# Layer 1 attention takes the value product of a batch one step later, behind the next scores; layer 0 folds its score scale into the latents

## Chip, cores and metric

One core of one Trainium2 chip runs the whole program: one launch, float32 inputs and outputs in HBM. The metric is the device time of a run in microseconds (us), and its median over several runs. The engines are called PE (matrix products; PEld is its load of stationary weights), DVE (VectorE), ACT (ScalarE), POOL (GpSimd) and SP (it issues the DMAs).

## The reference, cut to what matters

Two transformer layers after each other on a float32 stream x; each adds attention, normalises, adds a feed-forward part and normalises. The change touches the two attentions.

```python
# layer 0: 4 x 256 tokens, 32 heads, keys and values from a latent of 64, no mask
q  = (x @ Wq_c.T + bq_c) @ Wq_up.T + bq_up          # 192 latents for the queries
kv = x @ Wkv_c.T + bkv_c                            # 64 latents and 64 rope columns
scores = einsum(q, [kv_nope @ Wk_up.T, kv_rope]) / sqrt(192)
out = softmax(scores) @ v ; out = out @ Wo.T + bo
# layer 1: 4 batches x 256 tokens, 32 heads of 128, causal mask
q, k, v = x @ wq, x @ wk, x @ wv                    # per head 128 columns
scores = where(causal, q @ k.T * 192**-0.5, -1e30)
out = (softmax(scores) @ v) @ wo
```

The reference's causal mask is over 256 tokens of a batch, so of a batch's four 128 x 128 blocks of scores three are computed.

## The kernel before, in words

Every float32 operand of PE is split into a part `hi` rounded to fp32r and a rest `lo`, and a product is three matmuls (`matmul3`, L106 to L108): hi x hi, lo x hi, hi x lo. A split takes ACT for `hi` and DVE (or POOL) for `lo`. All engines have a queue of their own, in an order that is written out by hand, and meet by counting semaphores.

**Layer 0.** `attention0_heads` goes through 32 heads in rounds of four (one per batch); heads 2 to 26 run in a loop. For each head PE first multiplies the up-projection of queries and keys together (`merge`, two small float32 products in PSUM bank `bq`, L900). DVE then scaled the bank by 1/sqrt(192) into SBUF tile `gm` (`merged_raw`, L745), POOL scaled the rope columns into the other half of `gm` (`rope_part`, L603), ACT rounded `gm` to `gm_hi` (`merged`, L665) and DVE took `gm_lo` (`merged_lo`, L759). PE's `query` (L106 to L108, L913, L914) multiplies these weights with the query latents into `bq`; ACT and DVE split its result (`h_q_hi` L670, `h_q_lo` L763). Scores (`h_bs`) are products with the split latents `a_kv`. In the prologue the order is: latents, `merge(0)`, `query(0)`, scores, `merge(1)`.

**Layer 1.** `Attention1.programs` runs 32 heads x 4 batches = 128 steps s = 4h + t. Heads go in quads q (0 to 7); u = 0 to 15 is the step within a quad. Quads 1 to 6 are one hardware loop (`Fori`), quads 0 and 7 stand apart. In step s PE did, in this order:

1. scores of s+1 (five matmuls into `c_bs`, L106 to L108, L2462, L2463),
2. `turn`: three transposes of the probabilities of s (`c_bt`, L75), which wait for ACT's `normalise` of s (L1962),
3. products of the next head (`c_bx`, `c_by`), of the next quad's values (`c_bv`, `c_bw`: v1 to v7) and of the output projection,
4. values of s (five matmuls into `c_bo`, L106 to L108, L2481, L2483), which wait for the `lo` split of the probabilities (L2147) and for the value weights `c_v_lo` (`corner_lo`, L2178).

DVE's order in step s was: `out_sum(s-1)` (L2153, adds two halves of the output in `c_bo`), some of the value splits (`corner_lo`), `maxes(s+1)` (L2131, L2132, L2135, L2137, L2139), `outs(s-1)` (L2160), `probs(s)` (L2147), `inverse(s+1)` (L2143), then sums of the products. ACT's order was: `out_rest(s-1)` (L1972), value splits `corner_hi` (L2003), `probs(s)` (L1967), `outs(s-1)` (L1978, waits for `out_sum(s-1)`), value splits and copies `value_copy` (L2003, L1993), `exps(s+1)` (L1954, waits for `maxes`), copies of products (L2009), `normalise(s+1)` (L1962), `sum_hi` (L2016). PE's product v6 of a quad's second value pair stands in step u = 0 and waits for `value_copy(.., 0)`, v7 in u = 1 for `value_copy(.., 1)`.

The functions that the diff touches follow.

Of the kernel before, what the change touches and what calls it, by code (L numbers as in the profile page):

```python
# [34 lines left out]
ALU = mybir.AluOpType  # L35
# [178 lines left out]
class Latents0:  # L214
# [103 lines left out]
    def latent_hi(self, act, i):  # L318
# [4 lines left out]
        if m == 2:  # L323
# [4 lines left out]
            act.activation(self.kv[0][:, tok], self.kvraw[:, tok], ACT.Identity).then_inc(self.s_hi, 1)  # L328
# [5 lines left out]
    def latent_lo(self, dve, i):  # L334
# [94 lines left out]
def attention0_heads(nc, k, io, g, lat, acc, first, tail, norm, ffn, after, attn1, layer1):  # L429
# [13 lines left out]
    with ExitStack() as ctx:  # L443
# [7 lines left out]
        gm = t.sb("gm", [P, 2, P])  # L451
# [17 lines left out]
        s_gmm, s_graw, s_gpool, s_ghi, s_glo = (k.sem(x) for x in ("g_mm", "g_raw", "g_pool", "g_hi", "g_lo"))  # L469
# [52 lines left out]
        def merged_weights(h):  # L522
            i = tail_index(h)
            return (gms, gb) if i is None else (tail["gms"][i], tail["gb"][i])

# [18 lines left out]
        with nc.Block() as block:  # L544
# [49 lines left out]
            def _(pool):  # L594
                def rope_part(h):

                    _, _, rope, _ = weights(h)
                    loaded(pool, h)
# [60 lines left out]
            def _(act):  # L659
                def merged(h):  # L660
                    act.wait_ge(s_graw, h + 1)
                    act.wait_ge(s_gpool, h + 1)
                    if not is_late(h):
                        need(act, s_qmm, 2 * h)
                    act.activation(merged_weights(h)[0][0][:, :, :], gm[:, :, :], ACT.Identity).then_inc(s_ghi, 1)  # L665
# [58 lines left out]
                exps(0, 0)  # L724
                lat.latent_hi(act, 5)
                lat.rows_hi(act, 1)
                query(1, 1, 0)
                merged(1)
# [13 lines left out]
            def _(dve):  # L742
                def merged_raw(h):
                    dve.wait_ge(s_gmm, h + 1)
                    dve.tensor_scalar(gm[:, :, 0:KVL], bq[:, 0:2 * KVL].rearrange("p (a n) -> p a n", a=2), SCALE0,  # L745
                                      None, ALU.mult).then_inc(s_graw, 1)

                def merged_bias(h):
# [3 lines left out]
                    dve.scalar_tensor_tensor(out=terms[:, :], in0=factors[:, 0, :], scalar=SCALE0,  # L752
# [3 lines left out]
                def merged_lo(h):  # L756
                    hi, lo = merged_weights(h)[0]
# [2376 lines left out]
```

## Time and profile before

| | us |
|---|---|
| median of 3 runs (lowest, highest) | 1400.92 (1398.64, 1401.22) |
| the profiled execution | 1398.13 |
| its span in the trace | 1396.1 |
| outside the span | 2.0 |

PE is busy 99% of the span, DVE 75%, ACT 65%, POOL 62%. Layer 0's attention takes the first 363 us of the span, its feed-forward part the time to 490, layer 1's attention that to about 1320, and the last feed-forward part the rest. The clock granted to PE is that of full speed throughout. A matmul is shown with the time from its start to its modelled end, so that neighbours overlap; what one costs is the distance from start to start.

### The profile page before, as it was taken

What the parts mean: (1) busy time and instruction counts of PE and PEld (TensorE: products, weight loads), DVE (VectorE), ACT (ScalarE), POOL (GpSimd) and SP (SyncE); (2) the same over time, 40 slices, a digit from 0 to 9 for tenths busy, and PEclk for the clock granted to TensorE, in tenths of its full rate; (3) what the DMA queues carried; (4) which work ended last, traced back from release to release, by engine and by line L of the source; (5) the groups of instructions that cost most, each with busy time, mean ns of one, the idle gap of its engine ahead of it and who ended that gap; (6) DMA issues with size and microseconds to landing.
All of it is one profiled execution on the core that took longest, in us unless ns stands there. A gap on an engine that the chain in (4) does not pass through costs nothing.

```text
span 1396.1 us, 29891 instructions
## 1 busy us (share of the span) xinstructions
PE 1381.8 (99%) x8601; PEld 1216.0 (87%) x8601; DVE 1046.3 (75%) x2570; ACT 905.1 (65%) x2487; POOL 859.9 (62%) x926
## 2 busy tenths in 40 slices
PE   9999999999999999999999999999999999999998
PEld 7899889988788889898898898898898898898887
DVE  5999999999878886667667667667667667667876
ACT  5888888888555566566566566576576566566621
POOL 3655555555131367886885885886886886885521
PEclk9999999999999999999999999999999999999999
DMA  5533333322344400111102102102102002101201
GB/s 193 166 97 93 100 93 96 97 71 56 110 143 140 147 16 31 61 32 61 45 18 64 42 16 73 33 16 75 30 16 75 30 16 75 30 16 44 86 16 46
DMA packets 61299, 93.00 MB, mean 67 GB/s; under 512 B 6176, under 2 KB 31520, under 8 KB 61216
## 3 DMA queue, kind: packets, MB, share of 16 engines
q1 hardware_dynamic: 61072, 91.93, 22.2%
q8 instruction: 31, 0.51, 0.1%
q14 instruction: 52, 0.43, 0.1%
q10 hardware_dynamic: 144, 0.13, 0.0%
HBM read 81.82 MB, written 2.10 MB: 60 GB/s over the span
## 4 chain that ended last, share of the span: by engine, by line
PE 86%; DVE 5%; issue 3%; POOL 3%; ACT 3%; DMA 0%; POOLq 0%; DVEq 0%; ACTq 0%; SPq 0%
PE h_bo L949 5%; PE c_bx L106 4%; PE c_bx L108 4%; PE c_bv L106 4%; PE c_bx L107 4%; PE c_bv L108 3%; PE c_bv L107 3%; PE h_bo L1452 3%; PE a_acc L1452 3%; PE c_by L106 3%; PE c_bw L106 3%; PE c_by L108 3%; PE c_by L107 3%; PE h_bt L75 3%; PE c_bw L108 3%
## 5 line engine op out<-in xcount | busy, mean ns | idle before, releaser
L623 POOL TENSOR_TENSOR h_pr<-h_pr,h_rinv 128x512 f32<-128x512 f32 x128 | 133.4, 1042 | 136.4 <-DVE h_rinv L774 134.1
L1879 POOL TENSOR_TENSOR c_qk<-g_y,c_qk 128x512 fp32r<-128x512 f32 x96 | 123.4, 1296 | 100.8 <-ACT c_qk L2016 94.1
L1677 POOL TENSOR_TENSOR b_sw_lo<-b_slots,b_sw_hi 128x512 fp32r<-128x512 f32 (+1 forms) x128 | 151.1, 1180 | 10.3
L1675 POOL CAST b_sw_hi<-b_slots 128x512 fp32r<-128x512 f32 (+1 forms) x128 | 73.9, 577 | 90.1 <-DMA b_slots<-in_w_qk 69.3
L676 ACT ACTIVATE h_pr<-h_bs,h_nmax 128x256 f32<-128x256 f32 x256 | 119.6, 481 | 2.5 <-DVE h_nmax L769 2.4
L1962 ACT ACTIVATE c_pr<-c_pr,c_rinv 128x128 f32<-128x128 f32 (+1 forms) x256 | 101.8, 448 | 13.3 <-DVE c_rinv L2143 13.3
L2016 ACT ACTIVATE c_qk<-g_y 128x512 fp32r<-128x512 f32 x96 | 60.1, 628 | 72.6 <-DVE g_y L2203 72.1
L2153 DVE TENSOR_TENSOR c_bo<-c_bo,g_wo 128x128 f32<-128x128 f32 x128 | 38.3, 299 | 84.1 <-ACT g_wo L1972 69.7
L1632 POOL TENSOR_TENSOR b_slots<-b_slots 128x256 f32<-128x256 f32 x128 | 96.1, 773 | 2.5
L1954 ACT ACTIVATE c_pr<-g_wo,c_nmax 128x128 f32<-128x128 f32 x128 | 51.5, 403 | 63.6 <-DVE c_nmax L2139 63.6
L769 DVE TENSOR_REDUCE h_nmax<-h_bs 128x2 f32<-128x512 f32 x128 | 87.5, 683 | 0.0
L778 DVE TENSOR_TENSOR h_pt_lo<-h_bt,h_pt_hi 128x512 fp32r<-128x512 f32 x128 | 87.1, 680 | 0.3
L1967 ACT ACTIVATE c_pt<-c_bt 128x384 fp32r<-128x384 f32 x128 | 62.7, 489 | 31.6 <-PE c_bt L75 30.3
L1972 ACT ACTIVATE g_wo<-c_bo 128x128 f32<-128x128 f32 x128 | 34.5, 270 | 72.3 <-PE c_bo L2483 72.3
L106 PE MATMUL c_bx<-b_ts,b_sw_hi 128*128 128x512 f32 x192 | 78.9, 411 | 0.2
L682 ACT ACTIVATE h_pt_hi<-h_bt 128x512 fp32r<-128x512 f32 x128 | 76.4, 597 | 0.0
L106 PE MATMUL h_bs<-a_kv_hi,h_q_hi 128*128 128x256 f32 x256 | 74.6, 292 | 0.9 <-ACT h_pr L676 0.5
L108 PE MATMUL c_bx<-b_ts,b_sw_lo 128*128 128x512 f32 x192 | 75.4, 393 | 0.0
L949 PE MATMUL h_bo<-h_pt_hi,a_cs 128*128 128x256 f32 x252 | 75.1, 320 | 0.3 <-DVE h_o_mix L783 0.2
L107 PE MATMUL c_bx<-b_ts,b_sw_hi 128*128 128x512 f32 x192 | 75.0, 390 | 0.0
L75 PEld LDWEIGHTS h_bt<-g_ident,h_pr_t 128*128 128x128 f32 x512 | 54.9, 140 | 20.3 <-issue 7.8
L108 PE MATMUL h_bs<-a_kv_hi,h_q_lo 128*128 128x256 f32 x256 | 71.7, 280 | 0.0
(521 smaller groups left out, 5472.6 us busy)
## 6 DMA issues: line engine op xcount, KB each, us to landing
f_wi<-in_w_ffn SPq DMA_DIRECT2D x66, 256.0 KB, 2.7
b_slots<-in_w_qk SPq DMA_DIRECT2D x64, 256.0 KB, 3.0
a_w<-in_w_head SPq DMA_DIRECT2D x28, 352.0 KB, 3.0
h_part<-in_w_ffn SPq DMA_DIRECT2D x32, 264.0 KB, 2.7
h_o_mix<-h_o_hi SPq DMA_DIRECT2D x62, 128.0 KB, 2.2
b_vw_lo_raw<-in_w_v SPq DMA_DIRECT2D x9, 512.0 KB, 4.7
c_v_raw<-in_w_o SPq DMA_DIRECT2D x8, 512.0 KB, 4.1
g_xT_raw<-in_w_o SPq DMA_DIRECT2D x8, 512.0 KB, 4.0
```

What stands on the lines that cost most here:

```text
L75: return pe.transpose(out.bitcast(F32R), rows, ident)
L106: pe.matmul(out, w[0], x[0], start=start, stop=False, skip_group_check=True)
L107: pe.matmul(out, w[0], x[1], start=False, stop=False, skip_group_check=True)
L108: return pe.matmul(out, w[1], x[0], start=False, stop=stop, skip_group_check=True)
L623: pool.tensor_tensor(pr[b][:, :, :], pr[b][:, :, :], rinv[b][:, :][:, :, None].to_broadcast([P, 2, S]), ALU.mult)\
L676: m = act.activation(pr[b][:, i, :], bs[b % 2][:, i * S:(i + 1) * S], ACT.Exp, bias=nmax[b][:, i:i + 1], accum_out=rsum[b][:, i:i + 1])
L769: dve.tensor_reduce(nmax[b][:, :], bs[b % 2][:, :].rearrange("p (a n) -> p a n", a=2), AX, ALU.max, negate=True).then_inc(s_max, 1)
L949: m = pe.matmul(out, cs[:, 2 * (2 * c + b % 2) + kt, :], pt[b][j][:, kt, :], start=(b % 2 == 0 and kt == 0 and j == 0), stop=(kt == 1 and ...
L1632: pool.tensor_tensor(slot(out), slot(a), slot(b), op).then_inc(self.s_comb, 1)
L1677: pool.tensor_tensor(self.sw[1][:, a:b], self.slots[:, a:b], f32(self.sw[0][:, a:b]), ALU.subtract)\
L1879: pool.tensor_tensor(lo, y[:, (0, 2, 1)[i], :], f32(hi), ALU.subtract).then_inc(s_sumlo, 1)
L1962: m = act.activation(x[:, cols], x[:, cols], ACT.Identity, scale=rinv[t % 2][:, i:i + 1])
```

## The change

Layer 1: values of s-1 stand in step s, behind scores(s+1) and ahead of the turn, in all quads but the last, and there for u = 0; from u = 1 of the last quad on the old order holds. Their wait for the value weights (`values_ready`) moves with them. DVE takes `maxes(s+1)` first and `out_sum(s-1)` behind them; `value_total(2q-1, 2)` (L2173) goes from the start of step u = 3 to the end of u = 2.

Layer 0: the scale 1/sqrt(192) is applied to the latents (ACT's `scale=`, DVE's `scalar_tensor_tensor`), so `merged_raw` and tile `gm` go; ACT and DVE split the bank `bq` itself (64 instead of 128 columns for each of the two halves), and POOL splits the rope columns with two instructions in place of one. PE's `query` waits for POOL too. Head 1 uses a tail head's buffers, and its merge is split earlier in the prologue.

```diff
-            act.activation(self.kv[0][:, tok], self.kvraw[:, tok], ACT.Identity).then_inc(self.s_hi, 1)
+            act.activation(self.kv[0][:, tok], self.kvraw[:, tok], ACT.Identity, scale=SCALE0).then_inc(self.s_hi, 1)
...
-            dve.tensor_tensor(self.kv[1][:, tok], self.kvraw[:, tok], f32(self.kv[0][:, tok]),
-                              ALU.subtract).then_inc(self.s_lo, 1)
+            dve.scalar_tensor_tensor(out=self.kv[1][:, tok], in0=self.kvraw[:, tok], scalar=SCALE0,
+                                     in1=f32(self.kv[0][:, tok]), op0=ALU.mult, op1=ALU.subtract)\
+               .then_inc(self.s_lo, 1)
...
+            if isinstance(h, int) and h == 1:
+                return tail["gms"][0], gb
...
-                    need(pool, s_glo, h)
                     if tail_index(h) is None and is_late(h):
-                        need(pool, s_qlo, 2 * h)
+                        need(pool, s_qmm, 2 * h)
+                    if isinstance(h, int) and h == TAIL0:
+                        pool.wait_ge(s_qmm, 4)
-                    pool.tensor_scalar(gm[:, :, KVL:P], rope, SCALE0, None, ALU.mult).then_inc(s_gpool, 1)
+                    pool.tensor_copy(hi, rope).then_inc(s_rope, 1)
+                    pool.wait_ge(s_rope, h + 1)
+                    pool.tensor_tensor(lo, rope, f32(hi), ALU.subtract).then_inc(s_gpool, 1)
...
-                    act.wait_ge(s_graw, h + 1)
-                    act.wait_ge(s_gpool, h + 1)
-                    if not is_late(h):
-                        need(act, s_qmm, 2 * h)
-                    act.activation(merged_weights(h)[0][0][:, :, :], gm[:, :, :], ACT.Identity).then_inc(s_ghi, 1)
+                    act.wait_ge(s_gmm, h + 1)
+                    act.activation(from_merge(merged_weights(h)[0][0]), merged_bank, ACT.Identity)\
+                       .then_inc(s_ghi, 1)
...
-                def merged_raw(h):
-                    dve.wait_ge(s_gmm, h + 1)
-                    dve.tensor_scalar(gm[:, :, 0:KVL], bq[:, 0:2 * KVL].rearrange("p (a n) -> p a n", a=2), SCALE0,
-                                      None, ALU.mult).then_inc(s_graw, 1)
...
-                    dve.tensor_tensor(lo[:, :, :], gm[:, :, :], f32(hi[:, :, :]), ALU.subtract).then_inc(s_glo, 1)
+                    dve.tensor_tensor(lo, merged_bank, f32(hi), ALU.subtract).then_inc(s_glo, 1)
...
                     pe.wait_ge(s_glo, h + 1)
+                    pe.wait_ge(s_gpool, h + 1)
...
-                    if has(s - 1, NSTEP):
+                    late = not is_last(q) or u == 0
+                    if has(s - 1, NSTEP) and not late:
                         out_sum(s - 1)
...
-                    if filled and u == 3:
-                        value_total(2 * q - 1, 2)
...
                     if has(s + 1, NSTEP):
                         maxes(s + 1, (t + 1) % 4)
+                    if has(s - 1, NSTEP) and late:
+                        out_sum(s - 1)
...
                     add(1)
+                    if filled and u == 2:
+                        value_total(2 * q - 1, 2)
...
                         scores(s + 1, (t + 1) % 4)
+                    if late and has(s - 1, NSTEP):
+                        if u == 0:
+                            pe.wait_ge(s_clo, corners(2 * q - 2, "22"))
+                        else:
+                            values_ready(q, u - 1)
+                        values(s - 1, (j - 1) % 4 if t == 0 else j, (t - 1) % 4)
...
-                    values(s, j, t)
+                    if is_last(q):
+                        values_ready(q, u)
+                        values(s, j, t)
```

## Rows read from the trace of the kernel before

**Rows 1.** The page, part 1: busy us (share) xinstructions.

```profile
PE 1381.8 (99%) x8601; PEld 1216.0 (87%) x8601; DVE 1046.3 (75%) x2570; ACT 905.1 (65%) x2487; POOL 859.9 (62%) x926
```

**Rows 2.** Busy time by windows: layer 0's loop, layer 1's loop.

```profile
100.00:200.00 100.00, 100.00 (x733) 90.07 (x733) 93.84 (x209) 83.43 (x247) 53.90 (x69) 1.00 0.36 95
...
700.00:800.00 100.00, 99.85 (x613) 88.55 (x612) 67.20 (x183) 63.02 (x181) 78.30 (x81) 1.00 0.12 38
```

**Rows 3.** Waits of PEld: us in total, times, longest.

```profile
PEld c_bo L106 <- DVE c_v_lo L2178: 3.9, 7, 0.6
```

**Rows 4.** Timeline 12 to 22.5: start us, us, engine, line, operation [idle before].

```profile
18.29 0.29 DVE L745 TENSOR_SCALAR h_gm<-h_bq 128x128 f32<-128x128 f32 x1
18.40 0.39 PE L108 MATMUL h_bt<-g_xT_hi,p_wlo 128*128 128x512 f32 x1
...
19.06 0.43 DVE L759 TENSOR_TENSOR h_gm_lo<-h_gm,h_gm_hi 128x256 fp32r<-128x256 f32 x1 [0.48 <-ACT h_gm_hi L665]
...
19.64 0.47 PE L106 MATMUL h_bq<-a_qa_hi,h_gm_hi 128*128 128x512 f32 x1 [0.85 <-DVE h_gm_lo L759]
```

**Rows 5.** The page, part 5: groups of instructions.

```profile
L2153 DVE TENSOR_TENSOR c_bo<-c_bo,g_wo 128x128 f32<-128x128 f32 x128 | 38.3, 299 | 84.1 <-ACT g_wo L1972 69.7
```

**Rows 6.** Timeline of a late prologue stretch, 22 to 46.

```profile
31.44 0.79 DVE L759 TENSOR_TENSOR h_gm_lo<-h_gm,h_gm_hi 128x256 fp32r<-128x256 f32 x1
...
35.56 0.35 PE L106 MATMUL h_bs<-a_kv_hi,h_q_hi 128*128 128x256 f32 x1 [0.32 <-ACT h_pr L676]
```

**Rows 7.** Timeline of layer 0's loop, 200 to 215.

```profile
201.23 0.53 POOL L603 TENSOR_SCALAR h_gm<-a_w 128x128 f32<-128x128 f32 x1
...
204.31 0.39 PE L106 MATMUL h_bq<-a_qa_hi,h_gm_hi 128*128 128x512 f32 x1
```

**Rows 8.** Timeline of a plain step of layer 1, 750 to 771.

```profile
755.26 0.28 PE L106 MATMUL c_bo<-c_pt,c_v_hi 128*128 128x256 f32 x1
...
755.79 0.33 PE L106 MATMUL c_bs<-c_qk 128*128 128x256 f32 x1
```

**Rows 9.** Timeline of step u = 3 of a quad; last row one quad later.

```profile
742.12 0.39 PE L108 MATMUL c_bw<-g_xT_hi,c_oT 128*128 128x512 f32 x1
...
742.66 0.38 PE L106 MATMUL c_bo<-c_pt,c_v_hi 128*128 128x256 f32 x1 [0.15 <-DVE c_v_lo L2178]
742.72 0.80 ACT L1962 ACTIVATE c_pr<-c_pr,c_rinv 128x128 f32<-128x128 f32 x2 [0.78 <-DVE c_rinv L2143]
...
743.87 0.41 PE L75 MATMUL c_bt<-g_ident,c_pr_t 128*128 128x128 f32 x3
...
845.87 0.39 PE L108 MATMUL c_bw<-g_xT_hi,c_oT 128*128 128x512 f32 x1
```

**Rows 10.** Timeline of steps u = 15 and u = 0, 812 to 829.

```profile
817.84 0.79 ACT L1962 ACTIVATE c_pr<-c_pr,c_rinv 128x128 f32<-128x128 f32 x2
...
819.17 0.41 PE L75 MATMUL c_bt<-g_ident,c_pr_t 128*128 128x128 f32 x3
...
821.12 0.30 DVE L2153 TENSOR_TENSOR c_bo<-c_bo,g_wo 128x128 f32<-128x128 f32 x1 [2.46 <-issue]
...
822.09 0.63 ACT L2003 ACTIVATE c_v_hi<-c_vy 128x512 fp32r<-128x512 f32 x1 [0.24 <-DVE c_vy L2173]
...
823.21 0.40 ACT L1954 ACTIVATE c_pr<-g_wo,c_nmax 128x128 f32<-128x128 f32 x1
...
825.04 0.28 PE L106 MATMUL c_bv<-b_vw_hi,b_ts 128*128 128x256 f32 x1
```

**Rows 11.** The end of quad 0: ACT and PE in time.

```profile
610.41 0.80 ACT L1962 ACTIVATE c_pr<-c_pr,c_rinv 128x128 f32<-128x128 f32 x2
...
611.26 0.46 PE L75 MATMUL c_bt<-g_ident,c_pr_t 128*128 128x128 f32 x3
```

**Rows 12.** The instructions of L2178: ns min/median/max, first and last start.

```profile
L2178 DVE TENSOR_TENSOR c_v_lo<-g_y,c_v_hi x28: 691/786/1371, 594.0 to 1254.5; 128x512 fp32r<-128x512 f32 x28
L2178 DVE TENSOR_TENSOR c_v_lo<-c_bv,c_v_hi x14: 677/684/692, 610.5 to 1255.8; 128x512 fp32r<-128x512 f32 x14
```

More of the change, by code:

```diff
@@ L468, in attention0_heads @@
         s_w, s_wv, s_tick = first["w_in"], first["wv_in"], g["tick"]
-        s_gmm, s_graw, s_gpool, s_ghi, s_glo = (k.sem(x) for x in ("g_mm", "g_raw", "g_pool", "g_hi", "g_lo"))
+        s_gmm, s_rope, s_gpool, s_ghi, s_glo = (k.sem(x) for x in ("g_mm", "rope", "g_pool", "g_hi", "g_lo"))
         s_gb = k.sem("g_b")
@@ L523, in merged_weights, with from_merge, from_rope @@
             i = tail_index(h)
+            if isinstance(h, int) and h == 1:
+                return tail["gms"][0], gb
             return (gms, gb) if i is None else (tail["gms"][i], tail["gb"][i])
+        def from_merge(x):
+            return x[:, :, 0:KVL]
+        def from_rope(x):
+            return x[:, :, KVL:P]
+        merged_bank = bq[:, 0:2 * KVL].rearrange("p (a n) -> p a n", a=2)
         def loaded(eng, h):
@@ L751, in merged_bias @@
                         need(dve, s_qlo, 2 * h)
-                    dve.scalar_tensor_tensor(out=terms[:, :], in0=factors[:, 0, :], scalar=SCALE0,
+                    dve.scalar_tensor_tensor(out=terms[:, :], in0=factors[:, 0, :], scalar=1.0,
                                              in1=factors[:, 1, :], op0=ALU.mult, op1=ALU.mult,
@@ L756, in merged_lo @@
                 def merged_lo(h):
-                    hi, lo = merged_weights(h)[0]
+                    hi, lo = (from_merge(x) for x in merged_weights(h)[0])
                     dve.wait_ge(s_ghi, h + 1)
-                    dve.tensor_tensor(lo[:, :, :], gm[:, :, :], f32(hi[:, :, :]), ALU.subtract).then_inc(s_glo, 1)
+                    dve.tensor_tensor(lo, merged_bank, f32(hi), ALU.subtract).then_inc(s_glo, 1)
                 def query(p, par, h):
@@ L798, in round_ @@
                         maxes(s, b)
-                    if is_late(fresh):
-                        merged_raw(fresh)
                     if isinstance(s, int) and s == 1:
@@ L861, in _ @@
                     lat.latent_lo(dve, i)
-                merged_raw(0)
                 merged_lo(0)
@@ L869, in _ @@
                 maxes(0, 0)
-                merged_raw(1)
                 inverse(0, 0)
+                merged_lo(1)
                 lat.latent_lo(dve, 5)
@@ L874, in _ @@
                 query(1, 1, 0)
-                merged_lo(1)
                 lat.rows_lo(dve, 1)
@@ L2563, in v3, with values_ready @@
                     value_product(to, self.VS4, tokens(1, 1), pair, bw, False, s_vy)
+                def values_ready(q, u):
+                    head, b = divmod(u, 4)
+                    if is_first(q):
+                        pe.wait_ge(s_clo, (NB if head >= 2 else 0) + b + 1)
+                    else:
+                        which = ("11", "12", "21", "22")[head // 2 * 2 + b // 2]
+                        pe.wait_ge(s_clo, corners(2 * q - 2 + b % 2, which))
                 for t in range(NB):
                     s, u = 4 * h + t, 4 * j + t
+                    late = not is_last(q) or u == 0
                     if has(s + 1, NSTEP):
@@ L2573, in unit @@
                         scores(s + 1, (t + 1) % 4)
+                    if late and has(s - 1, NSTEP):
+                        if u == 0:
+                            pe.wait_ge(s_clo, corners(2 * q - 2, "22"))
+                        else:
+                            values_ready(q, u - 1)
+                        values(s - 1, (j - 1) % 4 if t == 0 else j, (t - 1) % 4)
                     ahead = isinstance(s, int) and s == 0
@@ L2644, in unit @@
                             out_last(i)
-                    if is_first(q):
-                        pe.wait_ge(s_clo, (NB if j >= 2 else 0) + t + 1)
-                    else:
-                        pe.wait_ge(s_clo, corners(2 * q - 2 + t % 2, ("11", "12", "21", "22")[j // 2 * 2 + t // 2]))
-                    values(s, j, t)
+                    if is_last(q):
+                        values_ready(q, u)
+                        values(s, j, t)
             def epilogue():
```

6 lines of the change are left out of this document (3 added, 3 removed).

## The prediction

> **What bounds the kernel now.** First the page's part 1 [rows 1]: PE is busy 1381.8 of 1396.1 us, so at most 14.3 us of the span are open gaps, and no edit here takes a matmul away or adds one. Then busy time by windows [rows 2]: PE fills 100.00 of 100 us in layer 0's loop and 99.85 in layer 1's. DVE is at 94 and 67, ACT at 83 and 63. Work taken from DVE or ACT is therefore worth nothing by itself; only a wait of PE pays. The views of waits name two that this change can reach. One stands before layer 0's first query: 0.85 us for DVE's `gm_lo` [rows 4]. The other comes seven times, once in each of the quads 1 to 7: the weights of the value product wait for `c_v_lo`, 3.9 us in all for the weight load [rows 3]. What such a wait costs PE is read from starts [rows 9]: the last product before it starts at 742.12 and a 512-column matmul takes 0.23 from start to start, so the values were due at 742.35; they start at 742.66 and, slowed by the late load, lose 0.1 more: 0.42 us a quad. Third, the timeline around each place, to see what is queued behind what.
>
> **Layer 0, the first query.** `gm_lo` ended at 19.49 and PE started at 19.64; its chunk ended at 18.40 + 0.23 = 18.63 [rows 4]. DVE reached `merged_raw` at 18.29, with its latent splits behind it. Now ACT can round the bank long before that, and DVE goes from 18.29 (a few hundredths later, as one latent split becomes the three-operand form) straight to `merged_lo`, on 128 elements a partition from PSUM: 0.30 by the nearest row [rows 5], so it ends at 18.65 and PE starts at 18.80. Gain 0.84. PE is the bound from there on (the next wait of the prologue stands behind ACT's split of a query, which moves along), so it is kept. ACT's instruction there gets smaller too, off this path.
>
> **Layer 0, the rest.** Head 1's `gm_lo` took 0.79 at 31.44, between a query's split and the maxima that later rounds wait for [rows 6]; the new order does it some 5 us sooner, when DVE is idle. PE loses about 1.2 us in short waits from 35 to 51, of which the 0.32 before 35.56 for the exponentials is one [rows 6]. Part of them sits behind ACT's split of a query, which waits for PE itself. I take 0.4, bounds 0 and 1.2. In the loop nothing is won: POOL's rope part takes 0.53 at 201.23 and the query needs it at 204.31 [rows 7]. Two instructions in place of one, 0.53 each at most and a semaphore between, are ready by 202.5; they no longer wait for DVE's query split. DVE's saving of 0.29 + 0.1 a head stands where it waits for PE anyway.
>
> A rule bears on the 0.79. The Trainium skill (SBUF — State Buffer, "SBUF: two separate sides") says that a DVE instruction with two SBUF inputs and a POOL one that reads SBUF lock each other out of a shared port pair for the whole instruction. By that rule, the new `merged_lo`, with one input in PSUM, is never held up; the trace agrees so far as the 0.79 stands against 0.43 at 19.06. The sum would be the same.
>
> **Layer 1: what the swap does to PE.** Values cost 755.79 - 755.26 = 0.53 [rows 8], and scores 0.59. Scores now start 0.53 sooner, values 0.59 later, the turn when it did. The corner's weights get 0.59 us more, against a wait of 0.42: the stall at u = 3 can go. That is the gain on offer: quads 1 to 6, 6 x 0.42 = 2.5 us (quad 7 keeps the old order there).
>
> **What it does to DVE and ACT.** `out_sum(s-1)` now stands behind `maxes(s+1)`, and ACT's `outs(s-1)` waits for it. ACT's queue is in order, so what stands behind `outs`, value copies and `exps(s+1)`, starts only after maxima + 0.30 (out_sum) + 0.04 + 0.30 (outs): 0.64 after the maxima instead of 0.04, so 0.6 later. In a plain step DVE waited for the scores, and their 0.53 gives that back: nothing is lost. It isn't given back where DVE waits for something else:
>
> - u = 15: DVE waits for ACT's `corner_hi("22")` ahead of the maxima. `exps`, `corner_hi("21")`, `corner_lo("21")` and `normalise` come about 0.52 later (0.6, less the slack that ACT has before the maxima's end). `normalise` ended at 818.63 and the turn started at 819.17 [rows 10]: 0.54 to spare, so even.
> - u = 0: after the loop's end DVE's next instruction came at 821.12, 2.46 after the last [rows 10]; now it comes 0.52 later, at 821.64. From 821.12 to the exponentials at 823.21 lay out_sum (0.25 of DVE's time), value_total and the maxima (1.8) and 0.04; so the maxima end at 823.44. out_sum 0.30 less an overlap of 0.08, 0.04 and outs 0.30: 824.00. Only then come ACT's `corner_hi("12")` and value copy, which ran beside the maxima before and took 823.21 - 822.09 = 1.12: the copy ends at 825.12. PE's product v6 was due at 825.04 [rows 10]. With 0.05 of semaphore: a new wait of 0.15. `exps` start at 825.1 instead of 823.21; I estimate that this just meets the next turn.
> - u = 1: inherits about 1.1, adds its own 0.6 and the copy in front; v7's copy ends just when PE comes: 0.1.
> - u = 2: PE's pace catches up; 0.02.
> - u = 3: value_total has gone, so the maxima start 0.7 sooner, but outs and `corner_hi("12")` now follow them. `c_v_lo`, `inverse` and `normalise` end 0.45 later. `normalise` ended at 743.52 [rows 9], so now at 743.97, and the turn starts at 744.02. In place of 743.87: 0.15 later per quad, with the stall of 0.42 gone and the three small ones in.
>
> So one wait is traded for four: +0.15 x 6 = +0.9. Quad 7's u = 0 gets v6's wait and keeps its old stall: +0.2. At the end of quad 0 `normalise` ends at 611.21 and the turn starts at 611.26, with nothing to spare [rows 11]; 0.52 later there is +0.5. Inside quad 0 the turns are as before.
>
> Bounds for a quad: -0.42 if the four new waits are nil; upwards, `c_v_lo` with both inputs in SBUF takes 0.69 to 1.37, while the one from PSUM never goes over 0.69 [rows 12]. What POOL does beside it is worth up to 0.68, and where I let it run free (u = 0) it may not be: +0.15 + 0.68 = +0.83.
>
> **Sum.** -0.84 - 0.4 + 0.9 + 0.2 + 0.5 = +0.4 us on the profiled execution's 1398.13. That run lies 2.8 below the median of the three, so I set the change against the median: 1401.3.
>
> **Rivals.**
> - *The stall goes and nothing comes in its place.* DVE's slack in u = 0 and u = 1 is larger than I make it, for instance if its 2.46 us at the loop's end shrink when it arrives later. -0.84 - 0.8 - 2.5 + 0.2 = -3.9: 1397.0. For it: the waits that I estimate are of 0.02 to 0.3 us, and each rests on a chain of some eight durations. Against: the order of ACT's queue, which holds whatever the durations are.
> - *Slower: POOL blocks `c_v_lo` at u = 0 or 3 for a whole instruction*, with exps and normalise behind it. It decides once `c_v_lo` ends over 0.3 us later than I have it in every quad. 6 x 0.83 = 5.0, with +0.2 + 0.5 - 1.24: +4.5, so 1405.4. For it: 1.37 is in the trace; against: the other engine's instruction must start just before, and the median is 0.79 [rows 12].
> - *No effect in layer 1.* Values and scores both wait for things that were mostly ready, so the swap may be idle and the corner's stall reappear at the next turn, to the same amount. Then only layer 0 shows: -1.2, 1399.7.
>
> **Chances and range.** My sum 0.35, no effect in layer 1 0.18, stall gone 0.25, POOL's block 0.22. A measurement of this kernel can tell about 0.2% (2.8 us) from no change. The first two lie within it, with little outside: faster 0.27, same 0.51, slower 0.22. The range runs from the stall-gone case, 1397, to near the blocked one, 1405.
>
> **What would show it.** After: no PE wait for `gm_lo` at 19 us, query some 0.8 earlier; no wait of `c_bo` for `c_v_lo` in quads 1 to 6 and one left in quad 7; exps 0.6 after the last maximum instead of 0.04, ACT waiting for `c_bo L2153` ahead of `outs`; new PE waits in u = 0 and 1 (`c_bv` for ACT's copy) and at the turn of u = 4. The loop's period was 103.8 us a quad (742.12 to 845.87, the same product in two quads [rows 9]); I expect 103.9 to 104.0. It is wrong if that period falls by 0.3 or more, or rises by over 0.5.

## The result and the profile after

| | before | after |
|---|---|---|
| median, us (lowest, highest) | 1399.45 (1397.33, 1401.22), 6 runs | 1406.28 (1405.41, 1408.2), 6 runs |
| profiled execution | 1398.13 | 1408.2 |
| its span | 1396.1 | 1406.2 |

The ratio is 1.0056, 95% interval 1.0046 to 1.0067: **slower by 0.56%**, 6.8 us by the medians. The prediction was 1401.3 in a range of 1397 to 1405. It missed, on the side of too little harm, and by more than the two times show: the median that I started from, 1400.92, lay 1.5 above that of the six runs, so the change was forecast at +0.4 and is +6.8.

The page of the changed kernel, parts 1 and 3 (part 3: packets, MB, share), with the one line of the kernel before that answers to the last, behind it. Most lines of layer 1 stand 4 further down than in the kernel before.

```profile
PE 1385.9 (99%) x8601; PEld 1214.9 (86%) x8601; DVE 1030.0 (73%) x2538; ACT 890.1 (63%) x2487; POOL 867.3 (62%) x958
...
q14 instruction: 77, 0.63, 0.1%
```

```profile
q14 instruction: 52, 0.43, 0.1%
```

DVE and ACT have less to do than in [rows 1], and the kernel is slower: the work taken away stood beside PE. What is new is on queue 14, which fetches instructions: 25 packets more, 0.20 MB.

Waits of PE and of its weight load in layer 1 (us in total, times, longest), changed kernel:

```profile
PE c_bw L106 <- DVE c_vy L2177: 3.6, 5, 0.8
PE c_bs L106 <- issue: 0.9, 1, 0.9
PE c_bv L106 <- ACT c_vy L1997: 0.4, 1, 0.4
```

```profile
PEld c_bs L106 <- DVE c_qk L2213: 2.9, 6, 0.5
PEld c_bv L106 <- ACT c_vy L1997: 2.2, 6, 0.9
PEld c_bt L75 <- ACT c_pr L1966: 2.1, 9, 0.4
...
PEld c_bo L106 <- DVE c_v_lo L2182: 0.6, 1, 0.6
```

The corner's wait of [rows 3] is down from seven times to the one of quad 7, as forecast. The first line is the one that I had not seen coming: product v2, at u = 0, waits for `value_total(2q-2, 2)`, five times, as often as the loop returns. The third is v7 in quad 1. (The quoted expectations say TensorE for PE.)

The place where the loop returns, changed kernel (start, us, operation, [idle before]); [rows 10] is the same place before:

```profile
824.65 0.28 ACT L1976 ACTIVATE g_wo<-c_bo 128x128 f32<-128x128 f32 x1 [2.01 <-issue]
...
825.41 0.69 DVE L2177 TENSOR_TENSOR c_vy<-c_bw,c_vy 128x512 f32<-128x512 f32 x1 [3.22 <-issue]
826.23 0.38 PE L106 MATMUL c_bw<-b_vw_hi,g_xT_hi 128*128 128x256 f32 x1 [0.70 <-DVE c_vy L2177]
826.94 0.49 ACT L1971 ACTIVATE c_pt<-c_bt 128x384 fp32r<-128x384 f32 x1 [2.02 <-issue]
```

"issue" means that nothing in the profile holds the engine. DVE's 2.46 us have become 3.22, and ACT, which passed the loop's return without a gap before, stands still for 2.01 and 2.02 us.

Layer 0's first query is as forecast: `gm_lo` takes 0.29, and PE starts 0.90 us sooner than in [rows 4] (I had 0.84). PE keeps that lead through layer 0's attention (0.83 us at 183 us, 0.92 at 337), but layer 1's first value product starts 0.37 later than before, not sooner: the lead is gone by then. What took it was not looked for.

```profile
18.35 0.29 DVE L766 TENSOR_TENSOR h_gm_lo<-h_bq,h_gm_hi 128x128 fp32r<-128x128 f32 x1
...
18.74 0.47 PE L106 MATMUL h_bq<-a_qa_hi,h_gm_hi 128*128 128x512 f32 x1
```

**Quads.** From here on a quad's length is the time from its first value product to the next quad's (starts of `c_bo<-c_pt,c_v_hi` on PE); a wait of PE is the excess of a start-to-start distance over what the same pair of matmuls usually takes. Quads 1 to 5 end with the loop's return; their mean is shown.

| kernel | median | ratio to before (95% interval) | quad 0 | quads 1 to 5 | PE waits in a quad of 1 to 5 |
|---|---|---|---|---|---|
| before | 1399.45 | | 99.8 | 103.85 | u=3: 0.31 |
| changed | 1406.28 | 1.0056 (1.0046, 1.0067) | 100.9 | 105.35 | u=4: 0.49, u=7: 0.23, top: 0.74 to 1.00 |
| e1 layer 0 only | 1398.41 | 0.9999 (0.9989, 1.0009) | 99.8 | 103.87 | u=3: 0.30 |
| e2 layer 1 only | 1402.92 | 1.0027 (1.0017, 1.0037) | 100.7 | 104.73 | u=4: 0.48, u=7: 0.22, top: 0.24 |
| e3 layer 0 only, shifted | 1398.69 | 0.9997 (0.9988, 1.0006) | 99.6 | 104.04 | u=3: 0.31 |
| e4 changed, shifted | 1402.92 | 1.0027 (1.0017, 1.0037) | 100.3 | 104.68 | u=4: 0.5, u=7: 0.23, top: 0 to 0.35 |
| e5 v2 later | 1406.80 | 1.0044 (1.0030, 1.0058) | 100.8 | 105.38 | as changed, but v6: 0.78 to 0.92 |
| e6 v2 later, shifted | 1402.63 | 1.0017 (1.0008, 1.0026) | 100.3 | 104.70 | u=4: 0.47, u=7: 0.21 |
| e7 sum first, shifted | 1402.38 | 1.0017 (1.0008, 1.0026) | 100.3 | 104.54 | u=3: 0.39, u=4: 0.53, u=7: 0.22 |
| e8 late at u=3 only | 1398.66 | 0.9988 (0.9979, 0.9997) | 99.6 | 104.05 | u=3: 0.33 |
| e9 corner first | 1398.94 | 1.0003 (0.9994, 1.0012) | 100.9 | 104.03 | u=7: 0.23, top: 0 to 0.26 |
| e10 exps first | 1400.47 | 1.0013 (1.0004, 1.0022) | 100.0 | 103.62 | u=7: 0.21 |
| e11 corner, exps, v2 | 1399.76 | 1.0008 (0.9999, 1.0017) | 100.2 | 103.55 | u=7: 0.22 |
| e12 late at u=4 only | 1397.59 | 0.9995 (0.9986, 1.0004) | 99.6 | 103.81 | u=4: 0.31 |
| e13 ACT's code shifted | 1406.89 | 1.0059 (1.0046, 1.0073) | 101.1 | 105.27 | as changed |
| e14 DVE's code shifted | 1403.29 | 1.0037 (1.0023, 1.0050) | 100.6 | 104.50 | u=4: 0.47, u=7: 0.21, top: 0 to 0.37 |
| e15 repaired, shifted | 1395.62 | 0.9983 (0.9973, 0.9992) | 100.0 | 103.26 | none |
| e16 repaired | 1395.40 | 0.9975 (0.9966, 0.9984) | 100.4 | 103.49 | none (one quad 104.34) |
| e17 repaired, keys of quad 0 first | 1395.35 | 0.9978 (0.9968, 0.9987) | 100.1 | 103.76 | none (two quads of 104.5) |
| e18 value sum back, shifted | 1402.36 | 1.0031 (1.0019, 1.0042) | 100.7 | 104.45 | u=4: 0.49, u=7: 0.22, top: 0 to 0.25 |

"Before" was measured anew with each group of runs (medians of 1398.33 to 1400.12), so kernels of different groups are compared by their ratios.

In some executions one or two quads carry 0.5 to 0.9 us more at u = 15 or at the top; such a one is in e3, e8, e16, e17 and others, with every order. It stays unexplained.

### The profile page after: what moved, and what is told of

It is laid out like the page before. It is cut to its first block, busy times and chain, and to the rows that moved or that the text cites. A ratio compares the mean times of both kernels' runs of the same rounds, so it can differ in the third digit from the quotient of the medians.

```text
span 1406.2 us, 29858 instructions
## 1 busy us (share of the span) xinstructions
PE 1385.9 (99%) x8601; PEld 1214.9 (86%) x8601; DVE 1030.0 (73%) x2538; ACT 890.1 (63%) x2487; POOL 867.3 (62%) x958
## 4 chain that ended last, share of the span: by engine, by line
PE 83%; DVE 5%; issue 4%; ACT 4%; POOL 3%; DMA 1%; DVEq 0%; SPq 0%; POOLq 0%; ACTq 0%
PE h_bo L953 5%; PE c_bx L106 4%; PE c_bv L106 4%; PE c_bx L108 4%; PE c_bx L107 3%; PE c_bv L108 3%; PE c_bv L107 3%; PE c_bw L106 3%; PE c_bw L108 3%; PE c_bw L107 3%; PE c_by L106 3%; PE h_bt L75 3%; PE c_by L108 3%; PE a_acc L1456 3%; PE c_by L107 3%
## 5 line engine op out<-in xcount | busy, mean ns | idle before, releaser
L1982 ACT ACTIVATE c_oT<-c_bo 128x256 fp32r<-128x256 f32 x124 | 47.8, 386 | 67.4 <-DVE c_bo L2157 65.9
L2164 DVE TENSOR_TENSOR c_oT<-c_bo,c_oT 128x256 fp32r<-128x256 f32 x124 | 52.5, 424 | 51.1 <-ACT c_oT L1982 51.1
L2013 ACT ACTIVATE g_y<-c_bx 128x512 f32<-128x512 f32 x96 | 57.1, 595 | 24.3 <-PE c_bx L108 18.4
```

## The experiments

**Which half of the change.** Theory S: the new order of the steps costs. Theory P: the place of the code does, that is, at which instruction number of an engine's program the loop begins. Counted in the built programs, the layer 0 part takes 8 instructions each out of ACT's and of DVE's program ahead of layer 1's loop.

> The change's layer 0 part alone (the scale taken with the latents, the merge without its raw copy), layer 1 as before. The changed kernel lost 6.8 us; its trace shows, at each return of layer 1's loop, ScalarE idle for 2.0 and 2.3 us where it had not been idle before, VectorE's idle time grown from 2.46 to 3.3 us, and 10 instruction fetches of 8 KB in a period of 105.35 us instead of 5 in 103.75. Theory P (place of the code): the layer 0 part takes 8 instructions each out of ScalarE's and VectorE's programs ahead of layer 1's loop, and so shifts the loop against the fetched blocks. Then this kernel, too, shows ScalarE's new gaps and 10 fetches a period, and the median is 2 to 6 us above the kernel before. Theory S (order of the steps): the loss comes from layer 1's new order. Then this kernel shows 5 fetches and no gap on ScalarE, and lies 0 to 1.5 us below the kernel before.

> The change's layer 1 part alone (value product of a step behind the next step's scores, VectorE's maxima first, one value sum a step sooner), layer 0 as before. ScalarE's program then stands at its old place. Theory P: no gap on ScalarE at the loop's return, about 5 fetches a period, period 103.6 to 104.2 us, median within 2 us of the kernel before. Theory S: the period is 105.0 to 105.5 us as in the changed kernel, TensorE still waits 0.7 to 1.0 us for c_vy at the top of a quad, and the median is 6 to 9 us above the kernel before.

For e3 and e4, "shifted" is this edit, in ACT's and in DVE's prologue of layer 1:

```diff
                 copy(1, 0)
+                for _ in range(16):
+                    act.wait_ge(s_khi, 1)
...
                 inverse(0, 0)
+                for _ in range(16):
+                    dve.wait_ge(s_exp, 1)
```

(16 waits that have long been met; in the built program they are 8 instructions, two waits in each.)

> As the layer 0 part alone, with 16 waits that are long met (8 instructions) added to ScalarE's and to VectorE's program at the end of layer 1's prologue, so that layer 1's loop stands at the instruction number that it has in the kernel before. Theory P: ScalarE's gaps and the extra fetches of the layer 0 part alone are gone, and the median is 0 to 1.5 us below the kernel before, or level with it. Theory S: it is equal to the layer 0 part alone within 0.5 us, whichever way that goes.

> The changed kernel with the same 8 instructions of met waits added to ScalarE's and to VectorE's program ahead of layer 1's loop. Theory P: ScalarE's gaps at the loop's return are gone and the fetches fall from 10 to about 5 a period, VectorE's gap is back at 2.3 to 2.5 us, TensorE's wait for c_vy at the top of a quad falls from 0.9 to 0 to 0.3 us, the period is 103.6 to 104.2 us, and the median is 5 to 9 us below the changed kernel. Theory S: the period stays at 105.0 to 105.5 us and the median stays within 1 us of the changed kernel's 1406.3.

Both theories hold, one for each half. Eight instructions that do nothing made the changed kernel 3.4 us faster (1406.3 to 1402.9), and e2, with layer 0 as before, runs at the same 1402.9. The rest, 3.4 us over the kernel before, is the order. Layer 0's part alone shows ACT's gaps and 10 fetches a quad too (before: 5), but costs nothing: its quads are of 103.87, so with the old order PE does not wait for the engine that comes late. Its forecast gain of 1.2 us (medians: 1.15 and 0.87 under before) is less than these runs tell from none.

**Where the late engine is waited for.** v2 moved behind `p2`, a product of the next head, in the changed kernel and in the shifted one:

```diff
-                    if filled and u == 0:
-                        v2(q, 1)
...
                         (p2, p5, p3)[t](h + 1)
+                    if filled and u == 0:
+                        v2(q, 1)
```

> The changed kernel (its code at its own place, ScalarE's gaps kept) with one edit: TensorE's product v2 at the top of a quad stands behind p2 instead of ahead of it, some 1.3 us later. Shifting the code alone gave 3.4 us. Theory V: the price of the place of the code is paid at one wait, v2's for the last value sum of the quad before (0.74 to 1.00 us a quad, five times in the loop), and nowhere else. Then this edit gives back 4 to 6 us, to 1400.5 to 1402.5, with 10 fetches a period still in the trace, and c_vy's wait on TensorE is gone. Theory W: ScalarE's gaps also make the exponentials and so the turns late; then v2's wait goes but 0.3 to 0.6 us a quad come back at a turn (c_bt waiting for ScalarE's c_pr), and the median is 1403 to 1405.

> The changed kernel with the code shifted to its old place and v2 behind p2. With the shift alone 0.17 us a quad were left at v2 and 1402.9 us in all. Theory V: it falls by 0.17 x 7, to 1401.3 to 1402.2, and the rest of the loss (0.5 us a quad at the turn of the quad's fifth step, 0.23 us at the scores of its eighth, 0.18 us at its thirteenth) stands. A rival: the same 0.2 us comes back one product later, at v6's wait for the value copy, and the median does not move (within 0.5 us of 1402.9).

Theory V's gain did not come, and W's place was wrong: e5's quads are as long as the changed kernel's (105.38 and 105.35). The wait went to v6, next in line, which needs ACT's copy of v1:

```profile
933.08 0.38 PE L106 MATMUL c_bv<-b_vw_hi,b_ts 128*128 128x256 f32 x1 [0.73 <-ACT g_y L1997]
```

So the whole chain of the quad's top is late (DVE's total, the maxima, the output sum, then ACT's output copy, corner and value copy), and not one product.

**Whose code.** Only one engine's program shifted:

> The changed kernel with the 8 instructions of met waits in ScalarE's program alone. Theory 1 (ScalarE's program is the one that lies badly): its gaps of 2.0 and 2.3 us at the loop's return go, the fetches fall from 10 to 5 a period, TensorE's wait at the top of a quad falls from 0.9 to 0.2 us, and the median is that of the kernel shifted on both engines, 1402 to 1403.5. Theory 2 (VectorE's program is): nothing changes, 1405.5 to 1407, 10 fetches.

> The changed kernel with the 8 instructions in VectorE's program alone. Theory 1: 10 fetches and ScalarE's gaps stay, VectorE's gap stays at 3.2 to 3.3 us, since two engines that fetch at once wait longer; the median stays at 1405.5 to 1407. Theory 2: VectorE's gap is back at 2.4 to 2.5 us and the median at 1402 to 1403.5.

Theory 1, which I had favoured, fell. With ACT's shifted (first block) its gaps are gone, the packets are back at 52, and the time does not move; with DVE's shifted (second block) ACT keeps gaps of 1.73 and 1.80, queue 14 has 77 packets, and the 3.4 us are back.

```profile
821.39 0.28 ACT L1976 ACTIVATE g_wo<-c_bo 128x128 f32<-128x128 f32 x1
821.55 0.50 ACT L1971 ACTIVATE c_pt<-c_bt 128x384 fp32r<-128x384 f32 x1
824.09 0.69 DVE L2179 TENSOR_TENSOR c_vy<-c_bw,c_vy 128x512 f32<-128x512 f32 x1 [3.04 <-issue]
824.91 0.38 PE L106 MATMUL c_bw<-b_vw_hi,g_xT_hi 128*128 128x256 f32 x1 [0.51 <-DVE c_vy L2179]
```

```profile
821.36 0.28 ACT L1976 ACTIVATE g_wo<-c_bo 128x128 f32<-128x128 f32 x1 [1.73 <-issue]
821.58 0.69 DVE L2177 TENSOR_TENSOR c_vy<-c_bw,c_vy 128x512 f32<-128x512 f32 x1 [2.41 <-issue]
822.40 0.38 PE L106 MATMUL c_bw<-b_vw_hi,g_xT_hi 128*128 128x256 f32 x1
823.43 0.49 ACT L1971 ACTIVATE c_pt<-c_bt 128x384 fp32r<-128x384 f32 x1 [1.80 <-issue]
```

What costs is the 0.5 to 0.8 us that DVE's gap grows by. ACT's 3.5 to 4.3 us of standing still at each return and its extra fetches, by far the louder signal, lie where ACT has time.

**The turn of u = 4.** The value sum's place and the output sum's place, each taken back alone on the shifted kernel:

> The changed kernel, code shifted to its old place, with VectorE's output sum back ahead of the maxima, TensorE's new order kept. My step in the prediction: the sum behind the maxima makes ScalarE's output copies and exponentials about 0.6 us later. Theory A (the sum's place is the cause): the turn's wait of 0.5 us a quad goes, and the median falls to 1399 to 1401. Theory B (TensorE's order is the cause): the sum now waits for a value product that stands behind the scores, 0.8 to 0.9 us later than the maxima could have begun; maxima, exponentials and turns come that much later in every step, and the median rises by 2 to 40 us over 1402.9, depending on how many of the 128 steps have less slack than that.

> The changed kernel, code shifted to its old place, with one layer 1 edit undone: VectorE's third value sum stands again at the head of the fourth step instead of at the end of the third. It waits for the same product either way and in the trace it began right at that product's end in both, so its 0.67 us should stand in the same place: quads of 104.4 to 104.6 us and a median within 1 us of the shifted kernel's 1402.9. If the sooner sum is what makes the fourth step fit at all, then without it the maxima of the fourth step come 0.2 to 0.7 us later, TensorE waits that much more at the fifth step's turn, and the median is 1404 to 1408.

e7 came out between its theories: the wait at v2 gave way to one of 0.39 at the values of u = 3, the one at the turn stayed (0.53), and so did the time. e18 shows the value sum's move to be worth nothing, as its first theory had it. So neither edit by itself is the cause. The chain is read in the shifted kernel at u = 3:

```profile
845.37 0.27 DVE L2145 TENSOR_REDUCE c_nmax<-g_wo 128x1 f32<-128x128 f32 x1
845.56 0.28 DVE L2159 TENSOR_TENSOR c_bo<-c_bo,g_wo 128x128 f32<-128x128 f32 x1
845.88 0.39 ACT L1982 ACTIVATE c_oT<-c_bo 128x256 fp32r<-128x256 f32 x1 [0.74 <-DVE c_bo L2159]
846.16 0.62 ACT L2007 ACTIVATE c_v_hi<-c_vy 128x512 fp32r<-128x512 f32 x1
...
846.61 1.29 POOL L1681 TENSOR_TENSOR b_sw_lo<-b_slots,b_sw_hi 128x512 fp32r<-128x512 f32 x1
...
846.68 0.39 ACT L1958 ACTIVATE c_pr<-g_wo,c_nmax 128x128 f32<-128x128 f32 x1
...
847.11 1.35 DVE L2184 TENSOR_TENSOR c_v_lo<-c_vy,c_v_hi 128x512 fp32r<-128x512 f32 x1
...
848.38 0.15 DVE L2149 RECIPROCAL c_rinv<-c_rsum 128x2 f32<-128x2 f32 x1
...
848.56 0.80 ACT L1966 ACTIVATE c_pr<-c_pr,c_rinv 128x128 f32<-128x128 f32 x2 [0.94 <-DVE c_rinv L2149]
...
849.42 0.45 PE L75 MATMUL c_bt<-g_ident,c_pr_t 128*128 128x128 f32 x3
```

The maxima are done at 845.64, the exponentials start at 846.68: 1.04 later, 0.6 of it the output sum and copy, as forecast. Then `c_v_lo` takes 1.35 us, in each of the loop's quads, where it took 0.93 before. It starts 0.50 after a POOL instruction of 1.29 us on SBUF and ends 0.56 after that one. The reciprocal, queued behind it, keeps ACT's normalisation waiting 0.94 us, and the turn comes late.

Of the two, the late exponentials and the long `c_v_lo`, the turn waits for the second. In e7 the exponentials start 0.03 after the maxima:

```profile
845.34 0.28 DVE L2145 TENSOR_REDUCE c_nmax<-g_wo 128x1 f32<-128x128 f32 x1
...
845.65 0.40 ACT L1958 ACTIVATE c_pr<-g_wo,c_nmax 128x128 f32<-128x128 f32 x1 [0.20 <-DVE c_nmax L2145]
...
846.02 1.29 POOL L1681 TENSOR_TENSOR b_sw_lo<-b_slots,b_sw_hi 128x512 fp32r<-128x512 f32 x1
...
846.33 1.53 DVE L2184 TENSOR_TENSOR c_v_lo<-c_vy,c_v_hi 128x512 fp32r<-128x512 f32 x1
```

`c_v_lo` begins 0.31 into POOL's subtraction, takes 1.53 and ends 0.55 after it, and the turn starts 1.52 after POOL's end, as in the shifted kernel (847.90 to 849.42). In every quad of every kernel in which `c_v_lo` begins inside that instruction, 0.3, 0.5 or 0.9 us into it, it ends 0.55 after it, the kernel before included (1.29 from 844.50, and 0.93 from 845.41). In the kernel before, the turn of u = 4 came 1.81 after POOL's end, 0.4 of it the corner's stall, so PE alone would have come at 1.4; in the changed kernel it would come at 1.0 (1.51 less the wait of 0.49). Why PE and POOL stand closer now was not tried. The repair starts the corner ahead of POOL's subtraction and puts the reciprocal right behind the corner:

```diff
                     probs(s)
+                    if filled and u == 3:
+                        corner_hi(2 * q - 1, "12", 1)
...
                     if has(s - 1, NSTEP) and late:
                         out_sum(s - 1)
+                    if filled and u == 3:
+                        corner_lo(2 * q - 1, "12", 1)
+                        inverse(s + 1, (t + 1) % 4)
```

> The changed kernel, code shifted to its old place; in the fourth step of a filled quad ScalarE makes the corner's upper half in the 0.74 us in which it stood waiting for VectorE's output sum, and VectorE makes the corner's lower half and the reciprocal ahead of the output's remainder and the turned probabilities. If the 0.49 us a quad at the fifth step's turn is the chain maxima, output sum, output copy, exponentials, a 1.35 us corner, reciprocal, normalisation, then it is gone (7 quads, 3.4 us): quads of 104.0 to 104.1 us instead of 104.5, median 1399 to 1400.5. If the turn waits for something else (ScalarE's sheer load in that step), it moves by less than 1 us from the 1402.9 of the shifted kernel.

The turn's wait is gone in the six quads that had it, the corner's wait of quad 7 too, and the ratio to the kernel before falls from e4's 1.0027 to 1.0003, which is 3.4 us. In its trace `c_v_lo` starts ahead of POOL's work and takes 0.75; now the POOL instruction beside it is the long one, 1.08 for a cast that took 0.61:

```profile
844.13 0.75 DVE L2184 TENSOR_TENSOR c_v_lo<-c_vy,c_v_hi 128x512 fp32r<-128x512 f32 x1
...
844.28 1.08 POOL L1679 CAST b_sw_hi<-b_slots 128x512 fp32r<-128x512 f32 x1
```

Whichever starts first runs at its own speed, and the other is longer by most of what the first still has to run. `c_v_lo` takes 0.68 at the least, so 1.35 is 0.67 more, where POOL still had 0.79 to run at 847.11; POOL's cast is 0.47 longer, where DVE still had 0.60. With one input in PSUM (`c_bv`) the same split took at most 0.70 in every run. The Trainium skill (SBUF — State Buffer, "SBUF: two separate sides") says that a DVE instruction with two SBUF inputs and a POOL one that reads SBUF hold a shared port pair for a whole instruction, and that the later one is blocked. The traces agree up to 0.13 us: the later one is longer by that much less than a full block.

**The exponentials' place in ACT's queue, and one late step.**

```diff
                     if has(s + 1, NSTEP):
                         exps(s + 1, (t + 1) % 4)
+                    if has(s - 1, NSTEP):
+                        outs(s - 1, out_region(h - 1 if t == 0 else h, (j - 1) % 4 if t == 0 else j), (t - 1) % 4)
```

(the same call is taken away above, and on DVE it goes likewise behind `inverse`; e11 has also e9's and e6's edits)

> The changed kernel, code shifted to its old place; in every step ScalarE makes the exponentials of the next step before the output copy of the last, and VectorE the turned probabilities and the reciprocal before the output's remainder. If the output sum behind the maxima costs because ScalarE's queue holds the exponentials behind a copy that waits for it, then TensorE's 1.11 us for the keys in the first quad falls to under 0.5, the 0.59 us in the second and the 0.23 us at the eighth step's scores go or halve, and the median falls by 1.5 to 3.5 us to 1399.5 to 1401.5. Rival: the value product then waits for the output's remainder (c_bo waiting for c_oT), 0.1 us or more in many steps, and the median rises by 1 to 12 us.

> The three edits together (corner early in the fourth step, exponentials ahead of the output copy, v2 behind p2) on the changed and shifted kernel. If the waits listed are separate and each goes, the loop's quads come to 103.4 to 103.7 us (before 103.8, changed and shifted 104.5) and the median to 1396 to 1398.5, below the kernel before. If the chain behind them (VectorE's and ScalarE's work of one quad) is what is too long, each edit only moves the wait, and the median stays above 1400.

Quads 1 to 5 came to 103.62 and 103.55, under the kernel before, and the turn's wait is gone. That it is gone through the exponentials, as e10's theory has it, is not shown: e7 has them as soon and waits. But e10 also takes the output's remainder from ahead of `c_v_lo` on DVE, so that this starts ahead of POOL's subtraction and takes 0.84; now POOL's takes 1.64 in place of 1.29.

```profile
843.58 0.84 DVE L2184 TENSOR_TENSOR c_v_lo<-c_vy,c_v_hi 128x512 fp32r<-128x512 f32 x1
...
843.95 1.64 POOL L1681 TENSOR_TENSOR b_sw_lo<-b_slots,b_sw_hi 128x512 fp32r<-128x512 f32 x1
```

Quad 7, which has the old order, went from 80.5 us to 83.2 (first to last value product): a value product there waits 1.03 us for the output's remainder, the rival of e10. Quad 0's wait fell only from 1.11 to 0.89, and the one at u = 7 stayed at 0.22. So the exponentials may go first only where the value product is late.

> Layer 0 part kept and code at the old place; in layer 1 the value product of a step stands behind the next step's scores in one step of sixteen only, the third of each quad that follows a filled one, where it waited 0.3 to 0.4 us for a corner in the kernel before; everywhere else the order of the kernel before. If the new order gains only where that wait stood and costs elsewhere (0.5 us at the fifth step's turn, 0.23 at the eighth's scores, 0.18 and 0.17 at two more), then the period is 103.3 to 103.6 us (before 103.75, changed and shifted 104.5) and the median 1396.5 to 1398.5, 0.1 to 0.2% under the kernel before. If the fifth step's late turn follows from the late value product of the third (it stands one step ahead of it), then that wait is still there and the period is 103.7 to 104.0, the median 1398.5 to 1400.

> Layer 0 part kept, code at the old place, the order of the kernel before everywhere but at one place: the value product of the fourth step of a filled quad, the one that waits 0.31 us for its corner, stands behind the scores of the fifth step's successor, and there VectorE takes the maxima first. (The kernel with only one late product before this one had it a step too early, at a product that did not wait.) Theory A (the wait only moves): 0.31 us goes and 0.3 to 0.5 us comes at the fifth step's turn; quads of 103.7 to 104.1 us, median 1398 to 1400. Theory B (the turn's wait belongs to the late order of all steps): quads of 103.45 to 103.55, median 1396 to 1397.5.

```diff
-                    late = not is_last(q) or u == 0
+                    late = filled and u == 3      # e8; e12: u == 4
```

e8 moved the product of u = 2, which doesn't wait, so it tells only that one late step is harmless. e12 moved the one of u = 3: its 0.31 went and 0.31 came at the next turn, quads of 103.81. That is theory A, the wait only moves. The path is the one above: exponentials 0.03 after the maxima, `c_v_lo` of 1.53 that ends 0.55 after POOL's subtraction, the turn 1.51 after that. In the kernel before, the value product and the turn both stood behind this `c_v_lo`; e12 frees the first of them alone.

**The repaired kernel.** `late` steps have the exponentials first, the corner is early, v2 behind `p2`, and at u = 6 an output tile (`tile(0)`, a product of the output projection) goes behind the key's product:

```diff
-                    if t and u != 3:
+                    if t and u not in (3, 6):
                         tile(0)
...
-                    if u in (0, 3, 4, 12):
+                    if u in (0, 3, 4, 6, 12):
                         tile(0)
```

(and DVE makes the key's remainder, `key_lo`, ahead of that tile's sum, `add(0)`, there)

> The changed kernel, code at the old place, with the corner early in the fourth step, the exponentials ahead of the output copy in the steps with a late value product only (not in the last quad, where that cost 2.9 us), v2 behind p2, and in the seventh step of a quad TensorE's output tile between the key's product and the one after it, with VectorE's key remainder ahead of that tile's sum. If the 0.22 us at the eighth step's scores is TensorE's own order, it goes here, and the first quad's 0.9 to 1.1 us too: quads of 103.2 to 103.45 us, median 1393.5 to 1396.5, 0.2 to 0.35% under the kernel before. If VectorE's queue is what is late, the wait stays, quads of 103.5, median 1396 to 1398.

> The same repaired order with the code where the changed kernel has it (10 fetches a period, ScalarE's gaps). If the price of the place is paid at waits of the quad's top that the repaired order has not made looser (v6 waited 0.9 us behind ScalarE's copy with v2 moved), it is 0.6 to 0.9 us a quad over the shifted one, 3 to 4.5 us. If the exponentials ahead of the output copy bring ScalarE to the loop's return earlier, it is under 1.5 us in all.

> The repaired kernel with the code at the changed kernel's place, and in the first quad's seventh step ScalarE makes the key's upper half before the exponentials (it stood idle for 1.5 us while the key product was done, and made it 2.1 us after that product's end), VectorE its remainder right behind the turned probabilities. If ScalarE's queue is the cause, the 0.89 us wait at 33.4 us of the first quad is gone and that quad is 99.1 to 99.6 us instead of 100.0 to 100.4; the median is 0.5 to 1 us lower than 1395.5, which is about what a comparison can tell. If it is not, the wait stays.

The wait at u = 7 is gone: the key's remainder ends before PE comes for the scores.

```profile
860.23 0.69 DVE L2218 TENSOR_TENSOR c_qk<-c_bx,c_qk 128x512 fp32r<-128x512 f32 x1
...
861.78 0.39 PE L108 MATMUL c_by<-g_xT_hi,b_sw_lo 128*128 128x512 f32 x1
862.01 0.28 PE L106 MATMUL c_bs<-c_qk 128*128 128x256 f32 x1
```

It was PE's own order. The scores of u = 7 need a key that leaves PE two products earlier and takes 0.60 on ACT and 0.69 on DVE; the 0.53 of value product that used to stand between had moved behind the scores. e15 and e16 are 0.17% and 0.25% faster than the kernel before and as fast as each other, although e16's DVE has gaps of 3.0 to 3.4 us: in an order with room at the top of a quad the place of the code costs nothing. In e17 quad 0's 0.89 went, and 0.72 came 8 us later, for `c_v_lo` from POOL; the quad is no shorter.

## Why the prediction was wrong

- **Layer 0, first query (-0.84):** right, 0.90. The 0.4 of the rest did not come: the waits from 35 to 51 us are 0.8 in both traces, and PE is 0.83 ahead in the loop.
- **"DVE's next instruction came at 821.12, 2.46 after the last; now it comes 0.52 later":** the step that failed. It holds the 2.46 fixed and looks for the loser at v6 and the turn. The gap was 3.09 to 3.34 us in the changed kernel, because the layer 0 part had moved DVE's code by 8 instructions; and the first to lose was v2, which I had not listed. Before, `value_total` ended at 822.06 and v2 started at 822.29, 0.23 to spare:

```profile
821.37 0.69 DVE L2173 TENSOR_TENSOR c_vy<-c_bw,c_vy 128x512 f32<-128x512 f32 x1
...
822.29 0.28 PE L106 MATMUL c_bw<-b_vw_hi,g_xT_hi 128*128 128x256 f32 x1
```

0.5 of lateness and 0.5 to 0.8 of larger gap, less the 0.25 of the output sum, which no longer stands ahead, gave a wait of 0.74 to 1.00 (PE starts 0.13 after the sum's end, and its late weight load costs 0.1 more). My own 821.64 would have shown a small one: 821.64 + 0.69 is past 822.29. Removing the larger gap alone (e4, e14) leaves 0 to 0.37. Price of the missing term: 3.4 us.
- **The turn of u = 4 (0.3 a quad):** the place was right, the path was not. The exponentials are late, as forecast (1.04 after the maxima), but e7 and e12 have them 0.03 after and the turn waits all the same. It waits for `c_v_lo`, whose end is tied to POOL's, 0.55 after it; I had left it at 0.93 us, it took 1.35, and the wait was 0.49. That is the POOL rival's mechanism, at u = 3. I gave it 0.22 and priced it at up to 0.83 a quad. That my 0.3 is near 0.49 is luck. The time of that rival, 1405.4, is near the one measured, but half of the measured loss has the other cause, so that is luck too.
- **"The turn when it did":** values and scores changed places, and I followed only what the values gained. The scores lost the value product as cover for the key: 0.23 a quad at u = 7 and 1.11 in quad 0, neither in my sum; the 0.5 foreseen at the end of quad 0 was 0.62 in the changed kernel and nothing in e4.
- **v6 and v7 at u = 0 and 1 (0.15 and 0.1):** v7 lost 0.6 in quad 1 and about 0.1 in the others, through its late weight load; v6 waited nowhere on PE, as v2 had waited already.
- **The stall gone at u = 3 (-0.42):** gone, but worth nothing by itself. In e12 the turn, which waits for the same `c_v_lo`, took it over, 0.31 for 0.31.
- **No effect in layer 1, and stall gone with nothing in its place:** both refuted by e2 (ratio 1.0027, interval from 1.0017).

By the trace, quads 1 to 5 took 103.85 to 105.35, 1.5 x 5 = 7.5 us; quad 0 took 1.2. I had said that a period up by over 0.5 would prove the sum wrong; it did.

## To carry to other kernels

At a hardware loop's return look up, for every engine, how long it stands with nothing holding it and which product needs its first result, and treat that time as variable: here an edit far ahead, in other code, changed it by 0.5 to 0.8 us. Judge the gap by who waits for the engine and not by its length or by the number of fetches; a few instructions added or taken ahead of the loop, in one engine's program at a time, is a cheap test. When a product is moved behind another, list what it used to cover for the one that now comes sooner, and move what stands in the helpers' queues along with it. Where a DVE instruction keeps ending a fixed time after a POOL one, shortening the work ahead of it gains nothing until it starts first. With all that done here the same idea turned 0.56% slower into 0.25% faster.

## What the runs showed of the hardware

- Where a loop's code stands matters. Eight instructions ahead of it in ScalarE's program switch two stops of 1.3 to 2.8 us on and off; eight in VectorE's change its stop at the return from 2.3 to 2.7 us to 3.0 to 3.4, with a second one of 0.39 in the third step. Fetch packets for the whole run are 52 or 77, and they follow ScalarE's place. The Trainium skill (Runtime: NRT & Kernel Launch, "Instruction fetch mechanics") says that a taken branch whose target isn't held forces a fetch before execution goes on. The trace agrees in part: in e13 fetch packets start at 821.04 and 821.46, where VectorE's stop begins (821.05), but the later one is done at 822.24 and the stop lasts to 824.09. What fills the rest, and why VectorE's stop grows with no more packets, stays open. Which instruction number is the edge was not tried.
- A VectorE subtraction with both inputs in SBUF took 0.68 to 2.65 us in the changed kernel (0.68 to 1.27 before, the same instruction), and delayed a POOL cast from 0.61 to 1.08 in e9. Where it began inside POOL's subtraction of 1.29 us at u = 3, it ended 0.55 after that one's end, whether it began 0.3, 0.5 or 0.9 us into it.
